# Linear attention of a six-layer decoder: the phi product as two 64-row tiles, in an order one step deeper

## The chip, the cores and the metric

One NeuronCore of one Trainium2 chip runs the whole program. The metric is the device time of one execution in microseconds (us); the time of a kernel is the median of its runs.

## The reference, cut to what matters

A decoder of two blocks works on `x` with 16 sequences of 128 tokens and 128 features. Six layers follow each other, each with a layer norm before it and a residual after it: softmax self-attention, softmax cross-attention, a butterfly feed-forward, linear attention (`_L1_attn_ref`, the layer of this case), autocorrelation cross-attention, and a mixture of experts.

The linear attention has 8 heads of 64 features. It is a recurrence with a decay `g` per head:

```python
q = _phi(x @ W_Q.T); k = _phi(x @ W_K.T)      # _phi(u) = elu(u) + 1
v = x @ W_V.T                                 # all reshaped to (b, t, H=8, DK=64)
S = g4 * S + einsum('bhi,bhj->bhij', kt, vt)  # one step per token
z = g3 * z + kt
out = einsum('bhij,bhi->bhj', S, qt) / (sum(z * qt) + EPS)
...
gate = sigmoid(x @ W_g_w.T + W_g_b)
return (outputs * gate).reshape(b, t, H * DK) @ W_O.T
```

## The kernel before

The kernel computes the recurrence in closed form. For each sequence and head, `A[s, t] = phi_k[s] . phi_q[t]`, multiplied by a mask that holds `g^(t-s)` where t is at least s and zero elsewhere; the numerator is then a matmul of the masked `A` with `v`, to which a column of ones is added so that the denominator comes out as the 65th column.

The stage (`linear_attention`) walks over the 16 sequences, one per step. Everything is fp32. TensorE executes each fp32 matmul as two instructions (a transpose through the identity is one), so the counts in the rows are twice the counts in the code.

Features of two heads share the 128 partitions: head 2c is in rows 0 to 63 and head 2c+1 in rows 64 to 127 of chunk c. The phi product uses full 128-row matmuls: `phi_q` has a slot for each of the two heads, `[128, C4, 2, T]`, and the half of the rows that belongs to the other head stays zero from a memset at the start of the stage. So 4 matmuls of 256 moving columns give all 8 heads, and VectorE writes `phi_q` in two pieces of 64 rows.

Each engine has its own order, written out by hand, and semaphores tie them together. In step b TensorE does: `attend(b)` (the phi product), `turn(b+1)` (transpose of the normalised x), `numerator(b)`, `project_kq(b+1)`, `turn_y(b)` (transposes of the divided output), `project_v(b+1)`, `out(b)` (the output projection), `project_g(b+1)`. VectorE does: `decay(b)` (masking of A, two pieces), `divide(b)`, `gate(b)`, `phi(b+1)`, `prepare(b+2)` (layer norm), `finish(b)` (residual and statistics). ScalarE does the copies and activations of one step after the other: copy of nT, clip and exp for k, the same for q, copy of v, and four tanh for the gate.

The two PSUM banks 4 and 5 hold A, and after it the transposed y and the output projection (`bank_y, bank_z = core.bank[4:6]`); `attend(b)` therefore waits in its second half for `x_done` of step b-1. Banks 6 and 7 hold the numerators.

The mask is built in the first stage (`attention`), in the order of the heads, and multiplied by the triangle there. That stage is the source of some rows below too: in `shifted_scores` (L588) it multiplies operands of 32 rows each, four row groups in turn, each into a bank of its own.

Of the kernel before, what the change touches and what calls it, by code (L numbers as in the profile page):

```python
# [21 lines left out]
B = 16  # L22
T = 128
# [125 lines left out]
def attention(core, m, f, lin, a):  # L149
# [63 lines left out]
    with nc.Block() as block:  # L213
# [164 lines left out]
        def _(act):  # L378
# [458 lines left out]

class LinMem:
# [12 lines left out]
def linear_attention(core, m, au, a):  # L851
# [15 lines left out]
    bank_y, bank_z = core.bank[4:6]  # L867
# [6 lines left out]
    with ExitStack() as ctx:  # L874
# [8 lines left out]
        phi_q = sb("li_phi_q", [128, C4, 2, T])  # L883
# [7 lines left out]
        with nc.Block() as block:  # L891
# [5 lines left out]
            def _(dve):  # L897
                def prepare(b):
# [59 lines left out]
                prepare(0)  # L958
                dve.memset(phi_q[:, :, :, :], 0.0).then_inc(zeroed, 1)
# [3 lines left out]
                dve.wait_ge(zeroed, 2)  # L963
                phi(0)
                prepare(1)
                with dve.Fori(0, B // 2 - 1) as i:
                    step(2 * i)
                    step(2 * i + 1)
                step(B - 2, left=1)
                variance(core, dve, EARLY, next_var)  # L970
                step(B - 1, left=0)
                dve.wait_ge(stat, B)
# [8 lines left out]
            @block.scalar  # L981
            def _(act):
                def prepare(b, first=False):
                    act.wait_ge(turned, b + 1)
                    act.activation(nT[:, :], bank_v[:, 0:T], ACT.Copy).then_inc(n_copied, 1)
                    for i, (proj, bank, clip, ex) in enumerate(((k_proj, bank_k, clip_k, exp_k),
                                                                (q_proj, bank_q, clip_q, exp_q))):
# [4 lines left out]
                        act.activation(ex[:, :, :], clip[:, :, :], ACT.Exp, scale=-1.0).then_inc(raised, 1)  # L992
                    act.wait_ge(v_proj, b + 1)
                    if first:
                        act.wait_ge(zeroed, 2)
                    act.activation(v[:, :, 0:K4], bank_v[:, :].rearrange("p (h w) -> p h w", h=H4), ACT.Copy)\
                        .then_inc(v_copied, 1)
                    act.wait_ge(gate_proj, b + 1)
# [7 lines left out]
                prepare(0, first=True)  # L1006
                with act.Fori(1, B) as b:
                    prepare(b)

            @block.tensor  # L1010
            def _(pe):
                def turn(b):
                    pe.wait_ge(normed, b + 1)
# [21 lines left out]
                def attend(b, first=False):  # L1035
                    pe.wait_ge(phi_done, 3 * (b + 1))
                    for c in range(C4):
                        if c == C4 // 2 and not first:
                            pe.wait_ge(x_done, b)
                        mm = pe.matmul(bank_a[c // 2][:, 256 * (c % 2):256 * (c % 2) + 256], phi_k[:, c, :],  # L1040
                                       phi_q[:, c, :, :].rearrange("p r t -> p (r t)"), start=True, stop=True)
                        if c % 2:
                            mm.then_inc(a_done, 1)

                def numerator(b):
                    pe.wait_ge(v_copied, b + 1)
                    for h in range(H4):
                        if h % half == 0:
                            pe.wait_ge(decayed, 2 * b + h // half + 1)
                        i = h % half  # L1050
                        mm = pe.matmul(bank_num[h // half][:, i * V1:(i + 1) * V1], am[:, h, :], v[:, h, :],  # L1051
                                       start=True, stop=True)
# [16 lines left out]
                def step(b, first=False, last=False):  # L1069
                    attend(b, first)  # L1070
                    if not last:
                        pe.wait_ge(v_copied, b + 1)
                        turn(b + 1)
                    numerator(b)
                    if not last:
                        project_kq(b + 1)
                    turn_y(b)
                    if not last:
                        project_v(b + 1)
                    out(b)  # L1080
                    if not last:
                        project_g(b + 1)

                pe.wait_ge(m.loaded, 80)
                turn(0)
                project_kq(0)
                project_v(0)
                project_g(0, first=True)
                step(0, first=True)
                with pe.Fori(1, B - 1) as b:  # L1090
                    step(b)
                step(B - 1, last=True)
# [1010 lines left out]
```

## Time and profile before

| what | value |
|---|---|
| median of 3 runs | 612.64 us (612.61, 612.64, 618.45) |
| the profiled execution's own time | 617.73 us |
| its span, first to last instruction | 615.6 us |
| busy TensorE, VectorE, ScalarE, GpSimd, of the span | 79%, 56%, 39%, 34% |
| mean granted TensorE clock | 0.875 |

The span is 2.1 us shorter than the profiled execution's own time; the rest lies around the first and last instruction. The profiled execution is 5.1 us above the median, and near to the third run. In the rows, "PE" is TensorE's matmuls, "PEld" its weight loads, "DVE" VectorE, "ACT" ScalarE. A granted clock of 1.00 is 2.4 GHz and 0.50 is 1.2 GHz.

### The profile page before, as it was taken

To read this page: it belongs to the slowest core of one execution; us is meant where nothing else is said; L and a number is where in the kernel's file an instruction comes from. 1 tells how busy PE (TensorE), PEld (TensorE's weight loads), DVE (VectorE), ACT (ScalarE), POOL (GpSimd) and SP (SyncE) were. 2 spreads that over 40 slices of the span, in tenths; PEclk is the share of its full clock that TensorE was granted. 3 is DMA by queue.
4 is the path that set the end of the run, shared out by engine and by line. 5 is a ranking of instruction groups with operands and counts; after the bars stand their busy time and mean duration, and the time that the engine had idled before them with its cause. 6 is when DMAs were issued, how large, how long until landed. Compare 5 with 4: busy or idle time off the path is not lost. (4 is left out here: it accounts for less than half of the span.)

```text
span 615.6 us, 13186 instructions
## 1 busy us (share of the span) xinstructions
PE 485.4 (79%) x4975; PEld 383.4 (62%) x4975; DVE 345.1 (56%) x934; ACT 239.0 (39%) x514; POOL 209.2 (34%) x234
## 2 busy tenths in 40 slices
PE   3879999999977979999999997996275232399960
PEld 1567777777754767888888886875155221266640
DVE  6546777777653446667766764344783767211114
ACT  3756666666542325444543541221121000132313
POOL 3546777799132233000000002123621000447750
PEclk9799999999996989999999997997585555599995
DMA  8960312200000011000000001200006000324417
GB/s 234 394 260 4 113 64 73 68 4 2 4 1 1 0 36 44 1 0 0 0 0 0 0 0 25 63 17 0 1 7 199 1 0 0 94 63 126 121 33 205
DMA packets 31460, 34.71 MB, mean 56 GB/s; under 512 B 5561, under 2 KB 25078, under 8 KB 31288
## 3 DMA queue, kind: packets, MB, share of 16 engines
q1 hardware_dynamic: 29208, 29.50, 15.3%
q0 software_dynamic: 2064, 4.60, 2.3%
q8 instruction: 31, 0.51, 0.4%
q14 instruction: 13, 0.11, 0.1%
q10 hardware_dynamic: 144, 0.00, 0.0%
HBM read 28.65 MB, written 5.46 MB: 55 GB/s over the span
## 5 line engine op out<-in xcount | busy, mean ns | idle before, releaser
L473 DVE TENSOR_REDUCE at_nmax<-bank 128x4 bf16<-128x512 f32 x128 | 82.5, 686 | 48.1 <-PE bank L569 48.1
L413 ACT ACTIVATE at_p<-bank 128x512 f32<-128x512 f32 x128 | 69.3, 597 | 38.2 <-PE bank L588 38.2
L95 POOL TENSOR_TENSOR var<-var,eps 128x12 f32<-128x12 f32 (+1 forms) x8 | 1.7, 206 | 191.1 <-DVE var L88 191.1
L1869 POOL DMA_INDIRECT mo_rows<-mo_n_rows,mo_src_row x24 | 23.0, 959 | 71.2 <-POOLq L1577 64.2
L582 PE MATMUL bank<-ident_b,at_nmax 128*128 128x128 bf16 x512 | 42.9, 222 | 3.9 <-DVE at_nmax L473 3.4
L582 PEld LDWEIGHTS bank<-ident_b,at_nmax 128*128 128x128 bf16 x512 | 31.0, 98 | 18.8 <-issue 9.5
L608 PE MATMUL bank<-at_p,at_v 128*32 128x128 f32 x1024 | 35.0, 276 | 3.9 <-issue 3.0
L1942 ACT ACTIVATE mo_h<-bank,mo_b 128x308 f32<-128x308 f32 x32 | 16.5, 517 | 47.1 <-PE bank L1905 47.1
L1913 PE MATMUL bank<-mo_w,mo_h 128*128 128x128 f32 (+1 forms) x192 | 32.9, 294 | 1.3 <-ACT mo_h L1942 1.3
L1040 PE MATMUL bank<-li_phi_q,li_phi_k 128*128 128x256 f32 x128 | 31.9, 393 | 0.9 <-DVE li_phi_q L908 0.9
L1051 PEld LDWEIGHTS bank<-li_v,li_am 128*128 128x128 f32 x256 | 29.8, 192 | 3.7 <-DVE li_am L915 3.1
L1051 PE MATMUL bank<-li_v,li_am 128*128 128x65 f32 x256 | 31.7, 277 | 0.1
L1913 PEld LDWEIGHTS bank<-mo_w,mo_h 128*128 128x128 f32 (+1 forms) x192 | 24.0, 172 | 11.9 <-ACT mo_h L1942 5.3
L608 PEld LDWEIGHTS bank<-at_p,at_v 128*32 128x32 f32 x1024 | 26.2, 110 | 8.1 <-issue 3.3
L1961 DVE COPY mo_xT<-bank 128x308 f32<-128x308 f32 x8 | 3.8, 478 | 48.2 <-PE bank L1896 48.2
L1637 PE MATMUL bank<-ro_reached,ro_ones_b 128*128 128x56 bf16 x160 | 10.9, 228 | 24.0 <-DVE ro_reached L1733 24.0
L1877 POOL DMA_INDIRECT mo_planes<-mo_y,mo_dst_row x24 | 23.7, 986 | 16.9 <-DVE mo_y L1968 10.5
L282 POOL TENSOR_TENSOR at_k_j<-at_kT,at_mask 128x512 f32<-128x512 f32 x16 | 16.6, 1039 | 30.7 <-PE bank L588 27.5
L1040 PEld LDWEIGHTS bank<-li_phi_q,li_phi_k 128*128 128x128 f32 x128 | 23.0, 190 | 4.3 <-DVE li_phi_q L908 1.1
L1002 ACT ACTIVATE li_tanh<-bank,li_gate_bias 128x128 f32<-128x128 f32 x64 | 18.2, 367 | 19.2 <-PE bank L1018 19.1
L989 ACT ACTIVATE li_clip_k<-bank 128x512 f32<-128x512 f32 x16 | 9.6, 597 | 40.3 <-PE bank L1018 40.3
L1637 PEld LDWEIGHTS bank<-ro_reached,ro_ones_b 128*128 128x128 bf16 x160 | 8.2, 121 | 26.7 <-DVE ro_reached L1733 25.4
(279 smaller groups left out, 1214.5 us busy)
## 6 DMA issues: line engine op xcount, KB each, us to landing
fo_w<-in_up_stages SPq DMA_DIRECT2D x9, 512.0 KB, 9.3
fo_w<-in_down_stages SPq DMA_DIRECT2D x9, 512.0 KB, 4.7
at_k_ctx<-in_ctx_heads SPq DMA_DIRECT2D x1, 4096.0 KB, 21.5
mo_w<-in_L_ffn_W SPq DMA_DIRECT2D x16, 256.0 KB, 3.1
mo_planes<-ro_zeros POOLq DMA_DIRECT2D x1, 2048.0 KB, 9.1
mo_got<-mo_planes SPq DMA_DIRECT2D x8, 256.0 KB, 4.8
x<-in_x SPq DMA_DIRECT2D x4, 256.0 KB, 3.5
au_ctx<-in_ctx SPq DMA_DIRECT2D x4, 256.0 KB, 4.0
```

The source lines that it names most:

```text
L282: pool.tensor_tensor(m.k_j[:, s % K_SLOTS, :, :], over(m.kT[:, g % 2, s % Q, :], J), m.mask[:, :].unsqueeze(2).to_broadcast([D, J, T]), AL ...
L413: act.activation(m.p[:, s % 2, J * g:J * g + J, :], bank_t[g][:, :].rearrange("p (j t) -> p j t", j=J), ACT.Exp, scale=scale).then_inc(exp ...
L473: dve.tensor_reduce(m.nmax[:, J * g:J * g + J], bank_s[g % 2][:, :].rearrange("p (j t) -> p j t", j=J), AX.X, ALU.max, negate=True).then_i ...
L582: pe.matmul(bank_t[g][:, j * T:(j + 1) * T], m.nmax[:, h:h + 1].to_broadcast([T, T]), core.ident_b[:, :], start=(j == 0), stop=False, skip ...
L608: mm = pe.matmul(bank_o[32 * c:32 * c + 32, half * T:half * T + T], m.v[:, g % 2, s % Q, h, :], m.p[:, s % 2, h, :], start=(odd == 0), sto ...
L1002: ins = act.activation(tanh[:, c, :], bank_g[:, c * T:(c + 1) * T], ACT.Tanh, bias=m.gate_bias[:, c:c + 1], scale=0.5)
L1040: mm = pe.matmul(bank_a[c // 2][:, 256 * (c % 2):256 * (c % 2) + 256], phi_k[:, c, :], phi_q[:, c, :, :].rearrange("p r t -> p (r t)"), st ...
L1051: mm = pe.matmul(bank_num[h // half][:, i * V1:(i + 1) * V1], am[:, h, :], v[:, h, :], start=True, stop=True)
L1637: mm = pe.matmul(bank_c[:, 0:TRIALS * E6], ones_b[:, :], reached[:, b, :, :].rearrange("t j e -> t (j e)"), start=(b == 0), stop=(b == B - 1))
L1869: pool.indirect_dma_start(out=rows[0:m, e % 2, r, :], out_offset=None, in_=n_rows, in_offset=bass.IndirectOffsetOnAxis(ap=src_row[0:m, til ...
L1877: pool.indirect_dma_start(out=planes, out_offset=bass.IndirectOffsetOnAxis(ap=dst_row[0:m, tile:tile + 1], axis=0), in_=y[0:m, e % 2, r, : ...
L1913: mm = pe.matmul(bank_y[r][0:m, 0:D], h[:, c, at[r]:at[r] + m], w2[:, par, c, :], start=(c == 0), stop=(c == CH6 - 1))
```

## The change

`phi_q` loses its zero half. Each head has a matmul of its own whose two operands lie in 64 of the 128 rows, 8 matmuls of 128 moving columns in place of 4 of 256; the even heads (rows 0 to 63) go to bank 4 and the odd ones to bank 5, in turn. VectorE writes `phi_q` in one piece of 128 rows, and the memset of it is gone. The masked A, the mask (also where the first stage makes it) and the numerator's order follow the new slots: even heads first, then odd ones. A signals once instead of twice.

The order is one step deeper: the gating, the output projection and the residual of step b-1 are done in step b. TensorE: `attend(b)`, `out(b-1)`, `project_kq(b+1)`, `numerator(b)`, `project_v(b+1)`, `project_g(b+1)`, `turn_y(b)`, `turn(b+2)`. VectorE: `gate(b-1)`, `decay(b)`, `finish(b-1)`, `prepare(b+2)`, `phi_k_of(b+1)`, `divide(b)`, `phi_q_of(b+1)`. ScalarE copies nT of the next step ahead of the gate's tanh. y's transposes and the output projection move to banks 6 and 7, so the numerator now waits for `x_done`. VectorE's loop has one step per turn where it had two.

```diff
@@ attention, scalar
-                act.activation(lin.mask[:, h, :], lin.gap[:, :], ACT.Exp, scale=lin.decay[:, h:h + 1])\
+                act.activation(lin.mask[:, slot(h), :], lin.gap[:, :], ACT.Exp, scale=lin.decay[:, h:h + 1])\
@@
+def slot(h):
+    return (h % 2) * C4 + h // 2
@@ linear_attention
-    bank_y, bank_z = core.bank[4:6]
+    bank_y, bank_z = core.bank[6:8]
-        phi_q = sb("li_phi_q", [128, C4, 2, T])
+        phi_q = sb("li_phi_q", [128, C4, T])
@@ vector
-                def phi(b):
+                def phi_k_of(b):
                     dve.wait_ge(raised, 2 * b + 1)
                     dve.scalar_tensor_tensor(out=phi_k[:, :, :], in0=by_chunk(bank_k[:, :]), scalar=0.0,
                                              in1=exp_k[:, :, :], op0=ALU.max, op1=ALU.add).then_inc(phi_done, 1)
+                def phi_q_of(b):
                     dve.wait_ge(raised, 2 * b + 2)
-                    for r in range(2):
-                        rows = slice(64 * r, 64 * r + 64)
-                        dve.scalar_tensor_tensor(out=phi_q[rows, :, r, :], in0=by_chunk(bank_q[rows, :]), scalar=0.0,
-                                                 in1=exp_q[rows, :, :], op0=ALU.max, op1=ALU.add)\
-                            .then_inc(phi_done, 1)
+                    dve.scalar_tensor_tensor(out=phi_q[:, :, :], in0=by_chunk(bank_q[:, :]), scalar=0.0,
+                                             in1=exp_q[:, :, :], op0=ALU.max, op1=ALU.add).then_inc(phi_done, 1)
                 def decay(b):
+                    dve.wait_ge(a_done, b + 1)
                     for i in range(2):
-                        dve.wait_ge(a_done, 2 * b + i + 1)
...
-                def step(b, left=2):
+                def step(b, first=False, left=2):
+                    if not first:
+                        gate(b - 1)
                     decay(b)
-                    divide(b)
-                    gate(b)
-                    if left >= 1:
-                        phi(b + 1)
+                    if not first:
+                        finish(b - 1)
                     if left >= 2:
                         prepare(b + 2)
-                    finish(b)
-                dve.memset(phi_q[:, :, :, :], 0.0).then_inc(zeroed, 1)
+                    if left >= 1:
+                        phi_k_of(b + 1)
+                    divide(b)
+                    if left >= 1:
+                        phi_q_of(b + 1)
...
@@ tensor
-                def attend(b, first=False):
-                    pe.wait_ge(phi_done, 3 * (b + 1))
+                def attend(b):
+                    pe.wait_ge(phi_done, 2 * (b + 1))
                     for c in range(C4):
-                        if c == C4 // 2 and not first:
-                            pe.wait_ge(x_done, b)
-                        mm = pe.matmul(bank_a[c // 2][:, 256 * (c % 2):256 * (c % 2) + 256], phi_k[:, c, :],
-                                       phi_q[:, c, :, :].rearrange("p r t -> p (r t)"), start=True, stop=True)
-                        if c % 2:
-                            mm.then_inc(a_done, 1)
+                        for r in range(2):
+                            rows = slice(64 * r, 64 * r + 64)
+                            mm = pe.matmul(bank_a[r][:, c * T:(c + 1) * T], phi_k[rows, c, :], phi_q[rows, c, :],
+                                           start=True, stop=True)
+                    mm.then_inc(a_done, 1)
-                def numerator(b):
+                def numerator(b, first=False):
                     pe.wait_ge(v_copied, b + 1)
-                    for h in range(H4):
-                        if h % half == 0:
-                            pe.wait_ge(decayed, 2 * b + h // half + 1)
+                    if not first:
+                        pe.wait_ge(x_done, b)
+                    for r in range(2):
+                        pe.wait_ge(decayed, 2 * b + r + 1)
+                        for h in range(r, H4, 2):
...
+                def step(b, first=False, left=2):
+                    attend(b)
+                    if not first:
+                        out(b - 1)
+                    if left >= 1:
                         project_kq(b + 1)
+                    numerator(b, first)
+                    if left >= 1:
+                        project_v(b + 1)
+                        project_g(b + 1)
                     turn_y(b)
+                    if left >= 2:
+                        turn(b + 2)
```

## Rows read from the trace of the kernel before

**Rows 1.** The page: granted TensorE clock in 40 slices, in tenths of full speed.
```profile
PEclk9799999999996989999999997997585555599995
```

**Rows 2.** Busy time by window: linear attention, routing, experts; then clock, DMA share, GB/s.
```profile
226.00:379.00 153.00, 147.42 (x1008) 126.80 (x1008) 99.50 (x238) 69.19 (x161) 10.05 (x11) 0.97 0.03 8
...
470.00:530.00 60.00, 19.10 (x219) 15.01 (x217) 39.41 (x117) 2.39 (x4) 1.05 (x1) 0.50 0.07 22
530.00:616.00 86.00, 57.15 (x280) 37.61 (x280) 16.39 (x52) 21.66 (x48) 45.63 (x47) 0.84 0.39 111
```

**Rows 3.** Timeline of TensorE's matmuls, one step: start, length, engine, line, operation.
```profile
297.77 2.00 PE L1040 MATMUL bank<-li_phi_q,li_phi_k 128*128 128x256 f32 x8
299.60 0.27 PE L1014 MATMUL bank<-ident,li_n 128*128 128x128 f32 x1
299.71 1.98 PE L1051 MATMUL bank<-li_v,li_am 128*128 128x65 f32 x16
301.52 1.11 PE L1018 MATMUL bank<-li_nT,li_wk 128*128 128x128 f32 x8
302.46 1.06 PE L1018 MATMUL bank<-li_nT,li_wq 128*128 128x128 f32 x8
303.36 0.60 PE L1058 MATMUL bank<-ident,li_y 128*128 128x128 f32 x4
303.80 1.02 PE L1028 MATMUL bank<-li_wv,li_nT 128*128 128x512 f32 x2
304.74 1.16 PE L1065 MATMUL bank<-li_wo,li_yT 128*128 128x128 f32 x8
305.73 1.06 PE L1018 MATMUL bank<-li_nT,li_wg 128*128 128x128 f32 x8
306.65 0.92 PE L1040 MATMUL bank<-li_phi_q,li_phi_k 128*128 128x256 f32 x3
```

**Rows 4.** Timeline of VectorE in the same step.
```profile
299.80 0.69 DVE L915 TENSOR_TENSOR li_am<-bank,li_mask 128x512 f32<-128x512 f32 x1 [0.17 <-PE bank L1040]
301.72 0.23 DVE L923 TENSOR_SCALAR li_den<-bank 128x4 f32<-128x4 f32 x2 [1.23 <-PE bank L1051]
...
302.22 0.76 DVE L930 TENSOR_TENSOR li_y<-bank,li_inv 128x256 f32<-128x256 f32 x2
304.00 0.69 DVE L937 SCALAR_TENSOR_TENSOR li_yT<-li_tanh,bank 128x512 f32<-128x512 f32 x1 [1.02 <-PE bank L1058]
...
305.20 1.40 DVE L908 SCALAR_TENSOR_TENSOR li_phi_q<-bank,li_exp_q 64x512 f32<-64x512 f32 x2
```

**Rows 5.** Timeline of ScalarE in the same step.
```profile
304.44 0.63 ACT L992 ACTIVATE li_exp_q<-li_clip_q 128x512 f32<-128x512 f32 x1
```

**Rows 6.** Timeline of TensorE in the step that holds VectorE's loop boundary.
```profile
272.66 0.27 PE L1014 MATMUL bank<-ident,li_n 128*128 128x128 f32 x1
272.90 2.00 PE L1051 MATMUL bank<-li_v,li_am 128*128 128x65 f32 x16
```

**Rows 7.** Timeline of TensorE in the cross-attention, where row and column tiles are used.
```profile
152.03 1.27 PE L588 MATMUL bank<-at_q,at_k_ctx 32*128 32x128 f32 x32
153.23 1.08 PE L608 MATMUL bank<-at_p,at_v 128*32 128x128 f32 x32
154.24 0.33 PE L612 MATMUL bank<-ident,at_o 128*128 128x128 f32 x1
154.50 0.40 PE L569 MATMUL bank<-at_k_ctx,at_q 32*128 32x512 bf16 x2
```

**Rows 8.** Timeline at the start of the linear attention: the memset and the first phi product.
```profile
226.93 0.91 DVE L959 MEMSET li_phi_q<- 128x1024 f32 x1 [0.16 <-issue]
...
235.02 1.99 PE L1040 MATMUL bank<-li_phi_q,li_phi_k 128*128 128x256 f32 x8 [0.91 <-DVE li_phi_q L908]
```

**Rows 9.** Timeline at its end: the sixteenth phi product (its first instruction) and the last residual.
```profile
369.24 0.48 PE L1040 MATMUL bank<-li_phi_q,li_phi_k 128*128 128x256 f32 x1
...
377.89 0.29 DVE L943 TENSOR_TENSOR x<-bank,x 128x128 f32<-128x128 f32 x1 [1.86 <-PE bank L1065]
```

More of the change, by code:

```diff
@@ L897, in _, with prepare @@
             def _(dve):
-                def prepare(b):
+                def prepare(b, first=False):
+                    if not first:
+                        dve.wait_ge(turned, b)
                     normalise(core, dve, n[:, :], b).then_inc(normed, 1)
-                def phi(b):
+                def phi_k_of(b):
                     dve.wait_ge(raised, 2 * b + 1)
@@ L962, in _ @@
                 dve.wait_ge(s_rstd, 2)
-                dve.wait_ge(zeroed, 2)
-                phi(0)
+                dve.wait_ge(zeroed, 1)
+                phi_k_of(0)
                 prepare(1)
-                with dve.Fori(0, B // 2 - 1) as i:
-                    step(2 * i)
-                    step(2 * i + 1)
+                phi_q_of(0)
+                step(0, first=True)
+                with dve.Fori(1, B - 2) as b:
+                    step(b)
                 step(B - 2, left=1)
@@ L971, in _ @@
                 step(B - 1, left=0)
+                gate(B - 1)
+                finish(B - 1)
                 dve.wait_ge(stat, B)
@@ L982, in _, with turn, features @@
             def _(act):
-                def prepare(b, first=False):
+                def turn(b):
                     act.wait_ge(turned, b + 1)
                     act.activation(nT[:, :], bank_v[:, 0:T], ACT.Copy).then_inc(n_copied, 1)
+                def features(b):
                     for i, (proj, bank, clip, ex) in enumerate(((k_proj, bank_k, clip_k, exp_k),
@@ L992, in prepare, with values, gates @@
                         act.activation(ex[:, :, :], clip[:, :, :], ACT.Exp, scale=-1.0).then_inc(raised, 1)
+                def values(b, first=False):
                     act.wait_ge(v_proj, b + 1)
                     if first:
-                        act.wait_ge(zeroed, 2)
+                        act.wait_ge(zeroed, 1)
                     act.activation(v[:, :, 0:K4], bank_v[:, :].rearrange("p (h w) -> p h w", h=H4), ACT.Copy)\
                         .then_inc(v_copied, 1)
+                def gates(b, first=False):
                     act.wait_ge(gate_proj, b + 1)
@@ L1004, in prepare @@
                     ins.then_inc(tanhed, 1)
-                prepare(0, first=True)
-                with act.Fori(1, B) as b:
-                    prepare(b)
+                turn(0)
+                features(0)
+                values(0, first=True)
+                turn(1)
+                gates(0, first=True)
+                with act.Fori(1, B - 1) as b:
+                    features(b)
+                    values(b)
+                    turn(b + 1)
+                    gates(b)
+                features(B - 1)
+                values(B - 1)
+                gates(B - 1)
             @block.tensor
@@ L1012, in turn @@
                 def turn(b):
+                    pe.wait_ge(v_copied, b)
                     pe.wait_ge(normed, b + 1)
@@ L1033, in project_g @@
                     project(b, m.wg, bank_g, gate_proj)
-                def attend(b, first=False):
-                    pe.wait_ge(phi_done, 3 * (b + 1))
+                def attend(b):
+                    pe.wait_ge(phi_done, 2 * (b + 1))
                     for c in range(C4):
-                        if c == C4 // 2 and not first:
-                            pe.wait_ge(x_done, b)
-                        mm = pe.matmul(bank_a[c // 2][:, 256 * (c % 2):256 * (c % 2) + 256], phi_k[:, c, :],
-                                       phi_q[:, c, :, :].rearrange("p r t -> p (r t)"), start=True, stop=True)
-                        if c % 2:
-                            mm.then_inc(a_done, 1)
-                def numerator(b):
-                    pe.wait_ge(v_copied, b + 1)
-                    for h in range(H4):
-                        if h % half == 0:
-                            pe.wait_ge(decayed, 2 * b + h // half + 1)
-                        i = h % half
-                        mm = pe.matmul(bank_num[h // half][:, i * V1:(i + 1) * V1], am[:, h, :], v[:, h, :],
-                                       start=True, stop=True)
+                        for r in range(2):
[4 more added lines that the diff above has]
+                def numerator(b, first=False):
+                    pe.wait_ge(v_copied, b + 1)
+                    if not first:
[3 more added lines that the diff above has]
+                        for h in range(r, H4, 2):
+                            i = h % half
+                            mm = pe.matmul(bank_num[h // half][:, i * V1:(i + 1) * V1], am[:, slot(h), :], v[:, h, :],
+                                           start=True, stop=True)
                     mm.then_inc(num_done, 1)
@@ L1067, in out @@
                     mm.then_inc(out_done, 1)
[L1069 to L1075, printed above, removed]
+                def step(b, first=False, left=2):
+                    attend(b)
+                    if not first:
+                        out(b - 1)
+                    if left >= 1:
                         project_kq(b + 1)
+                    numerator(b, first)
+                    if left >= 1:
+                        project_v(b + 1)
+                        project_g(b + 1)
                     turn_y(b)
[L1078 to L1082, printed above, removed]
+                    if left >= 2:
+                        turn(b + 2)
                 pe.wait_ge(m.loaded, 80)
-                turn(0)
+                pe.wait_ge(normed, 1)
+                pe.transpose(bank_v[:, 0:T], n[:, :], core.ident[:, :]).then_inc(turned, 1)
                 project_kq(0)
@@ L1088, in _ @@
                 project_g(0, first=True)
+                turn(1)
                 step(0, first=True)
-                with pe.Fori(1, B - 1) as b:
+                with pe.Fori(1, B - 2) as b:
                     step(b)
-                step(B - 1, last=True)
+                step(B - 2, left=1)
+                step(B - 1, left=0)
+                out(B - 1)
 NH5 = 16
```

2 lines of the change are left out of this document (1 added, 1 removed).

## The prediction

> **What bounds the kernel now.** I read the windows by stage first. The changed stage lasts 153 us of 615.6, and TensorE is busy for 147.4 of them at a granted clock of 0.97, nearly all of it at the 2.4 GHz level [rows 2]. Then the timeline of TensorE in one steady step. The reader is to look at the starts, not at the lengths: the lengths overlap, and the distance from one start to the next is what TensorE spends. From one phi product to the next it is 306.65 - 297.77 = 8.88 us, made of 1.83 (phi product), 0.11 (turn), 1.81 (numerator), 0.94 + 0.90 (k, q), 0.44 (turn of y), 0.94 (v), 0.99 (out) and 0.92 (gate), with no hole in it [rows 3]. So TensorE's issue is the bound. What a deeper order alone can give back is small: the v projection streams 2 x 512 columns, which by the other rows' rate (0.112 for 128 columns) is 0.85, so 0.09 of its 0.94 is TensorE waiting for the gating (304.00 to 304.69, and the output projection starts at 304.74 [rows 3, 4]); out takes 0.99 where the equal q projection takes 0.90. Together 0.18 per step. In every second step the numerator starts 0.24 instead of 0.11 after the turn [rows 6]; that is the step with VectorE's loop boundary, where masking comes late. Over the stage, 15 steps from 235.02 to 369.24 [rows 8, 9] are 8.95 each, so this costs 0.07 in the mean.
>
> **The phi product.** Before: 8 instructions of 256 columns, 1.83, or 0.229 each. After: 16 instructions of 128 columns in 64 rows. No row of before shows a 64-row tile. Nearest is the 32-row tile of the cross-attention: 32 instructions, 128 fp32 columns each, and 1.20 us from their first to the next group, 0.0375 each [rows 7]; a full-height instruction of the same columns takes 0.112 [rows 3]. Four row groups in turn therefore do run beside each other. In that group each row tile has 32 / 4 = 8 instructions behind each other, as each of the two 64-row tiles will have (16 / 2). Free overlap would make it 8 x 0.112 = 0.90, the lower bound; the 32-row group takes 1.20, or 1.05 without the one change of tile shape in it (0.15, below). Upper bound, no overlap at all: 16 x 0.112 = 1.79. I take 1.00, nearest to the row, since two tiles have half as many instructions to issue as four.
>
> **The change of tile shape.** The new phi product stands between full-height matmuls, so each step has two changes of shape. The transpose L612 takes 0.26 to its successor, a 32-row tile [rows 7], while the transpose in the linear stage takes 0.11 [rows 3]: 0.15 for a change. I take 0.13 each, 0.26 per step; bounds 0 and 0.35. The Trainium skill, "TensorEngine Tiling (Array Packing)", Key Properties, says that changing the tiling mode, not just the tile, drains TensorE; this is the rule that speaks against the change, and the trace agrees, with the 0.15 above. The same skill, "TensorE: Matmul & The Clock Gate", Packing small matmuls, puts the further tiles of a packed group at about 4 ns each; by that the phi product would be near the floor of 0.90 and the total 1.5 us lower. The trace is above it: 1.05 for the 32-row group without its change, where 0.90 would be free.
>
> **TensorE's step after.** 8.88 - 1.83 - 0.18 + 1.00 + 0.26 = 8.13, against 8.95 in the mean. 0.82 saved, 15 steps: **12.3 us**.
>
> **Does anything else take its place?** I follow the new order with the rows' distances, counting from TensorE's end of the numerator. VectorE's divide starts 0.20 later and its y is done at 302.98, 1.46 after [rows 3, 4]. TensorE has v and gate to issue in that time, 0.85 + 0.92 = 1.77, so turn of y finds y ready with 0.3 to spare. Then phi_q, now one piece of 0.70 instead of two (1.40 [rows 4]), is done at about 2.15 plus some 0.05 of signalling; TensorE wants it after turn of y and turn, at 1.77 + 0.44 + 0.11 = 2.32. Slack 0.1: the tightest place. The output projection needs the gating: turn of y ends its issue at 2.21, its result reaches VectorE some 0.2 later, gating takes 0.69, so 3.15 against 2.32 + 1.26 = 3.58 for TensorE. Masking: a_done at about 3.8, two pieces of 0.69, 5.2; the numerator is reached at 3.58 + 0.90 + 1.84 = 6.3. The residual behind it is ready at 5.5 to 5.8. The exps for q end 3.6 after the k projection's start (305.07 - 301.52) [rows 3, 5], and VectorE takes them 3.65 + 1.46 = 5.1 after it. VectorE's loop boundary, now in each step, lies between phi_q and the gating, where 0.4 is free. v's copy is awaited by turn(b+2), with 0.5 free. The waits that change add none; behind a late phi_q would be the whole TensorE queue. The mask's new slots in the first stage, the other numbering of A and the two banks cost nothing: same instructions, same sizes. ScalarE's copy of nT is done 0.5 after turn; TensorE has phi product and out (2.2) in between.
>
> **The ends.** The first phi product waited for two pieces of phi_q and now for one: 0.7 earlier. The memset of 0.91 is gone, but the first phi_k waits for ScalarE long after it [rows 8], so nothing for that. Step 0 has no output projection: 0.9 less. The last step pays: before, from the sixteenth phi product to the last residual, 8.65 [rows 9]. Now out(14) lies in it, and the numerator waits for its residual, which stands behind two maskings on VectorE with nothing on TensorE to cover it: +1.0. Sum -0.6. **Total -12.9 us.** For the profiled execution that is a span of 602.7 and an own time of 604.8. The median is 5.1 below the profiled execution's time, and the rows don't say where that lies; I take the same 12.9 off the median: 612.64 - 12.9 = 599.7, say 600.
>
> **Rivals.**
> *A, the forecast:* tiles overlap, TensorE's issue stays the bound: 597 to 603.5. Lower end: phi product 0.90, changes 0.2: step 7.97, 2.4 below. Upper: 1.10 and 0.35, step 8.32, 2.9 above.
> *A', phi_q becomes the last to come.* If divide or phi_q is 0.3 later than counted (for instance two signals more), the loop of numerator, divide, phi_q, phi product, out, k and q is 8.4: 604. For it: slack is only 0.1. Against: each part is taken from a row.
> *B, the tiles don't overlap.* The phi product is 1.79 + 0.26, the step 8.92, the stage the same as before within 0.5 and the ends 0.6: 612. The change then doesn't do what it says, and the deeper order only pays for the shape changes. Against it: the 32-row rate; for it: weights of 64 rows and 128 columns are a form that no row shows.
> *C, slower.* Every change from one 64-row tile to the other costs what a change of shape costs. There are 7 inside the phi product: 7 x 0.15 = 1.05 on top of B gives a step of 9.97 and +15 us, 628. The point from which it decides: above 8.95 - 7.05 + 0.18 = 2.08 for the whole phi product with its changes, 0.13 per instruction, the change loses. Against it: L588 changes its row group every second instruction and takes 0.0375 each [rows 7].
> *D, the late stages take another clock.* Routing ran at 0.50 and the experts at 0.84 in the profile [rows 1, 2]; runs of one kernel differ by 5.8 us (612.61 to 618.45), which may be such a change. If most runs of the new kernel fall to that side, 600 + 5.8 = 606.
>
> **How the numbers follow.** A 0.65, A' 0.08, D (with A) 0.09, B 0.12, C 0.06. A measurement here tells about 1% (6.1 us) from no change. Faster by over 1% (below 606.5): A, A' and most of D, 0.80. Within 1%: B and the rest of D, 0.13. Slower: C and a little more, 0.07. The range reaches from A's lower end to D: 596.5 to 607; B and C are left out.
>
> **What would show it.** Right: starts of the phi product 8.0 to 8.3 apart with no wait in TensorE above 0.1; from the phi product's start to out's start 1.1 to 1.4; its matmuls in the form 64*128; VectorE waiting before the gating and before the divide, not TensorE. No alternation from step to step. Wrong: a TensorE wait on phi_q (A'); 1.9 or more from phi product to out (B), over 2.1 (C); a difference that lies behind the end of the stage (D).

## The result and the profile after

| | before | after |
|---|---|---|
| median of the runs beside each other | 613.15 us (612.61 to 618.45) | 599.51 us (598.51 to 600.22) |
| ratio | | 0.974, 95% interval 0.968 to 0.980 |
| profiled execution: own time, span | 617.73, 615.6 us | 599.32, 597.2 us |

The medians are 13.6 us apart, 2.2%; the ratio, which is not formed from the medians, gives 2.6%. The forecast was 600 us. The changed kernel was run again beside the later experiments: 599.98 us against 613.65, ratio 0.980 (0.975 to 0.984).

The windows of the changed kernel, from the profile of that second run (same columns as [rows 2]; linear attention, then routing and experts). The borders are those of [rows 2], 17.5 us earlier from the end of the changed stage on:

```profile
222.50:361.50 139.00, 134.25 (x1136) 120.12 (x1136) 86.06 (x222) 70.78 (x161) 10.13 (x11) 0.95 0.03 9
...
452.50:512.50 60.00, 19.19 (x220) 15.13 (x218) 39.42 (x117) 2.39 (x4) 1.04 (x1) 0.50 0.07 21
512.50:598.00 85.50, 57.24 (x280) 37.66 (x280) 16.41 (x52) 21.66 (x48) 45.62 (x48) 0.84 0.39 113
```

TensorE is still busy for nearly all of the changed stage. The late stages have the clocks that they had before (0.50 and 0.84).

One steady step of TensorE in the changed kernel's first profile; it answers to [rows 3]:

```profile
300.80 1.16 PE L1069 MATMUL bank<-li_phi_q,li_phi_k 64*128 64x128 f32 x16
301.89 1.16 PE L1095 MATMUL bank<-li_wo,li_yT 128*128 128x128 f32 x8
302.89 1.06 PE L1047 MATMUL bank<-li_nT,li_wk 128*128 128x128 f32 x8
303.78 1.06 PE L1047 MATMUL bank<-li_nT,li_wq 128*128 128x128 f32 x8
304.68 1.90 PE L1081 MATMUL bank<-li_v,li_am 128*128 128x65 f32 x16
306.41 1.08 PE L1057 MATMUL bank<-li_wv,li_nT 128*128 128x512 f32 x2
307.32 1.05 PE L1047 MATMUL bank<-li_nT,li_wg 128*128 128x128 f32 x8
308.21 0.60 PE L1088 MATMUL bank<-ident,li_y 128*128 128x128 f32 x4
308.65 0.27 PE L1043 MATMUL bank<-ident,li_n 128*128 128x128 f32 x1
308.85 0.49 PE L1069 MATMUL bank<-li_phi_q,li_phi_k 64*128 64x128 f32 x4
```

The step is 308.85 - 300.80 = 8.05 us, and so in 13 of the 15 steps (the first, without an output projection, is 7.16, and the last, without a turn, 7.94), where before it was 8.95 in the mean [rows 8, 9]. The phi product holds TensorE for 1.09 instead of 1.83. Look at the small differences as well. The numerator takes 1.73 and not 1.81, v 0.91 and not 0.94, gate 0.89 and not 0.92; there TensorE had waited a little in before. k takes 0.89 and not 0.94, but that was no wait. Taken singly, the first instruction of the group behind the numerator has 0.05 more to its successor than it has elsewhere: in before that group is k (0.16 where the others have 0.11), here it is v (0.48 where v's first had 0.43 in before). The 0.05 has only moved to another group.

On the other side, out takes 1.00 where q, the same amount of work, takes 0.90, and turn takes 0.20 where it took 0.11. Those two stand on either side of the 64-row tiles. Out took 0.99 in before too, behind a wait for the gating [rows 3, 4]; here it waits for nothing, and experiment 1 has it at 0.89 with full-height tiles and no wait.

VectorE around the same place; it answers to [rows 4]:

```profile
298.56 0.23 DVE L929 TENSOR_SCALAR li_den<-bank 128x4 f32<-128x4 f32 x2 [0.64 <-PE bank L1081]
...
299.06 0.76 DVE L936 TENSOR_TENSOR li_y<-bank,li_inv 128x256 f32<-128x256 f32 x2
299.74 0.68 DVE L915 SCALAR_TENSOR_TENSOR li_phi_q<-bank,li_exp_q 128x512 f32<-128x512 f32 x1
300.80 0.69 DVE L943 SCALAR_TENSOR_TENSOR li_yT<-li_tanh,bank 128x512 f32<-128x512 f32 x1 [0.39 <-PE bank L1088]
302.01 1.29 DVE L921 TENSOR_TENSOR li_am<-bank,li_mask 128x512 f32<-128x512 f32 x2 [0.52 <-PE bank L1069]
```

phi_q ends at 300.42 (299.74 + 0.68) and the phi product that needs it starts at 300.80. VectorE now waits for TensorE before the divide, the gating and the masking (the brackets), and TensorE waits for no one.

**Where the time went, by stretch.** From the first layer norm of the stage to that of the next stage, the first profile of before has 152.6 us (226.4 to 379.0), the changed kernel 137.9 (222.4 to 360.3) in its first profile and 139.0 in its second. Of that, the 15 steps between the sixteen phi products are 134.22 before and 119.76 after in both: -14.46. The stretch ahead of the first phi product is 8.6 before, 6.8 and 7.95 after; the first of these two ran its first projections at a granted clock of 1.00 and the second at 0.66 at the start, like before. The stretch behind the sixteenth is 9.8 before and 11.3 after. With the second profile, whose start has the clock of before, that is -14.46 - 0.67 + 1.5 = -13.6, the difference of the medians.

The spans of the two first profiles differ by 18.4, not by 13.6: 4.0 of it lie ahead of the changed stage, which begins at 226.4 and at 222.4. The change touches only the order of the mask's slots there, and two of the experiments, which do nothing else to that part, have the 4 us as well (last section).

### The profile page after: what moved, and what is told of

Same layout as the page of the kernel before. It is cut to its first block and busy times, and to the rows that moved or that the text cites. A ratio compares the mean times of both kernels' runs of the same rounds, so it can differ in the third digit from the quotient of the medians.

```text
span 597.2 us, 13480 instructions
## 1 busy us (share of the span) xinstructions
PE 469.0 (79%) x5103; PEld 374.5 (63%) x5103; DVE 332.1 (56%) x917; ACT 240.4 (40%) x514; POOL 209.2 (35%) x234
## 5 line engine op out<-in xcount | busy, mean ns | idle before, releaser
L1081 PE MATMUL bank<-li_v,li_am 128*128 128x65 f32 x256 | 30.4, 272 | 0.5 <-issue 0.5
L921 DVE TENSOR_TENSOR li_am<-bank,li_mask 128x512 f32<-128x512 f32 x32 | 20.6, 686 | 8.7 <-PE bank L1069 8.6
L1938 PE MATMUL bank<-mo_xT,mo_w 128*128 128x308 f32 x64 | 24.7, 492 | 0.6 <-DVE mo_xT L1994 0.6
L588 PE MATMUL bank<-at_q,at_k_j 32*128 32x128 f32 x512 | 21.6, 286 | 0.1
```

What stands on the lines that cost most here:

```text
L588: mm = pe.matmul(bank_t[g][:, j * T:(j + 1) * T], keys(s, g)[:, j, :], queries(s, g), start=False, stop=(j == J - 1), skip_group_check=True)
L921: dve.tensor_tensor(am[:, half * i:half * i + half, :], bank_a[i][:, :].rearrange("p (h t) -> p h t", h=half), m.mask[:, half * i:half * i ...
L1938: pe.matmul(bank_up[c % 2][:, 0:CAP], w1[:, par, c * 128:(c + 1) * 128], xT[:, :], start=True, stop=True).then_inc(up_done, 1)
```

## The experiments

Steps are distances between phi products, as above, from each kernel's profile.

**1. The order alone.** The old full-height product, with the zeros in phi_q and its two pieces, in the new order:

```diff
-                    dve.scalar_tensor_tensor(out=phi_q[:, :, :], in0=by_chunk(bank_q[:, :]), scalar=0.0, ...
+                    for r in range(2):
+                        rows = slice(64 * r, 64 * r + 64)
+                        dve.scalar_tensor_tensor(out=phi_q[rows, :, r, :], in0=by_chunk(bank_q[rows, :]), ...
...
+                        mm = pe.matmul(bank_a[c // 2][:, 256 * (c % 2):256 * (c % 2) + 256], phi_k[:, c, :],
+                                       phi_q[:, c, :, :].rearrange("p r t -> p (r t)"), start=True, stop=True)
```

> The deeper order with the old full-height phi product (phi_q with its zero half, written in two pieces). Theory 1 (each part needs the other): phi_q now stands behind the divide, and in two pieces it comes 0.7 us later than in the changed kernel, where it has 0.33 to spare; TensorE waits about 0.4 per step for it. Step 6.87 + 1.83 + 0.45 = 9.15 us against 8.95 before, time 615 to 617 us. Theory 2 (the parts add up, TensorE's issue bounds): the order alone gives back its 0.18 + 0.07 per step, step 8.70, time 609 to 610 us, no wait on phi_q.

Measured: 616.66 us against 613.9, ratio 1.006 (1.002 to 1.009). Step 9.07. The timeline of TensorE:

```profile
283.88 0.27 PE L1047 MATMUL bank<-ident,li_n 128*128 128x128 f32 x1
284.47 1.99 PE L1071 MATMUL bank<-li_phi_q,li_phi_k 128*128 128x256 f32 x8 [0.32 <-DVE li_phi_q L917]
286.30 1.05 PE L1098 MATMUL bank<-li_wo,li_yT 128*128 128x128 f32 x8
287.19 1.06 PE L1051 MATMUL bank<-li_nT,li_wk 128*128 128x128 f32 x8
```

Theory 1 holds: the deeper order without the one-piece phi_q makes the kernel slightly slower, since VectorE's second piece comes late in every step. This profile also gives the clean price of all the other work, with full-height tiles around it and no wait in it. From turn to the phi product it is 0.59, of which 0.11 are turn itself and 0.48 are lost; 9.07 - 1.83 - 0.48 = 6.76.

One thing stays open here. In every kernel with the full-height product, phi_q comes late or only just in time, and the product's first instruction has 0.32 to its successor where the others have 0.216. So up to 0.10 of the 1.83 may be lateness too; no kernel shows the full-height product with phi_q well ahead of it.

**2. The tiles alone.** The 64-row product and the one-piece phi_q in the old order:

```diff
+                    if not first:
+                        pe.wait_ge(x_done, b)
+                    for c in range(C4):
+                        for r in range(2):
+                            rows = slice(64 * r, 64 * r + 64)
+                            mm = pe.matmul(bank_a[r][:, c * T:(c + 1) * T], phi_k[rows, c, :], phi_q[rows, c, :],
+                                           start=True, stop=True)
+                    mm.then_inc(a_done, 1)
```

> The two 64-row tiles and the one-piece phi_q in the old order. Theory 1: the phi product is done 0.7 us sooner, but the numerator behind it has only one transpose as cover and waits for the masking: from the start of the phi product 1.21 to the mask, 0.69 for its first piece, so the numerator starts 1.94 after, as before. Step 8.88, time 610 to 613 us; the timeline shows TensorE waiting some 0.7 per step before the numerator. Theory 2 (parts add up): 1.83 becomes about 1.2, step 8.30, time 603 to 604 us, no such wait.

Measured: 614.54 us against 613.9, ratio 1.003 (0.999 to 1.006). Step 8.99.

```profile
284.88 1.16 PE L1043 MATMUL bank<-li_phi_q,li_phi_k 64*128 64x128 f32 x16
285.97 0.33 PE L1015 MATMUL bank<-ident,li_n 128*128 128x128 f32 x1
286.83 2.00 PE L1053 MATMUL bank<-li_v,li_am 128*128 128x65 f32 x16 [0.53 <-DVE li_am L917]
```

The phi product is as short as in the changed kernel (1.09), and all of it is given back at once: the numerator starts 1.95 after it, as it did in before (1.94 [rows 3]), because it waits for the masking. That is theory 1 in its mechanism; the step came out 0.11 longer than it said and the time above its 610 to 613, and 0.07 of that is the change of shape in front of the product (gate takes 0.99 here, 0.92 in before). So neither half of the change gains anything; both together gain 13.6 us. The order hides the masking, and phi_q in one piece comes early enough for the order to run without a wait.

**3. Where does 1.09 come from: two tiles beside each other, or cheaper matmuls?**

```diff
-                    for c in range(C4):
-                        for r in range(2):
+                    for r in range(2):
+                        for c in range(C4):
```

> The changed kernel with the phi product's matmuls in another order: the four of rows 0 to 63 first, then the four of rows 64 to 127. Theory 1 (the gain is two row tiles running beside each other, and TensorE issues in order): no overlap, 16 x 0.112 + 0.2 = 2.0 us per phi product in place of 1.09, step 8.95, time 612 to 614 us. Theory 2 (a 64-row matmul is simply cheaper): 1.09 stays, 599 to 600 us.

Measured: 608.5 us against 613.9, ratio 0.991 (0.988 to 0.994). Step 8.60.

```profile
297.75 1.71 PE L1069 MATMUL bank<-li_phi_q,li_phi_k 64*128 64x128 f32 x16
299.38 1.16 PE L1095 MATMUL bank<-li_wo,li_yT 128*128 128x128 f32 x8
```

1.63: neither theory. The same 16 instructions cost 0.54 more when the row group changes once instead of each time, so the gain is overlap and theory 2 falls. But it is 0.35 less than no overlap at all (16 x 0.112 + 0.19 = 1.98), so part of the second group ran beside the first.

The single records show which part. In the changed kernel the starts come in pairs, 0.006 apart, and the pairs follow each other by 0.112 (the first pair by 0.213). Here they begin 0, 0.214, 0.325, 0.437, 0.549 and then 0.555, 0.660, 0.768, 0.772: the fifth instruction of the first row group starts at 298.294, and one that is as long (0.37) as only the first of a row group is starts at 298.300. So the second row group began with three instructions of the first still to start, and 3 x 0.112 = 0.34 fits the 0.35. A record doesn't name its row group; I read it from the lengths and distances.

**4. The row group changes after every second matmul.**

```diff
-                    for c in range(C4):
-                        for r in range(2):
+                    for r, c in ((0, 0), (0, 1), (1, 0), (1, 1), (0, 2), (0, 3), (1, 2), (1, 3)):
```

> The changed kernel with the row group changing after every second matmul (two of rows 0 to 63, two of rows 64 to 127, and again), where the changed kernel alternates each time and the grouped variant changed once. The grouped product took 1.63 us, between 1.09 with full overlap and 2.0 with none. Theory 1 (TensorE starts matmuls of the other row group some instructions ahead of its turn, three in the grouped variant): three boundaries give enough overlap, the product stays at 1.1 to 1.2, step 8.05 to 8.15, time 599.5 to 601 us. Theory 2 (only the neighbouring matmul at a boundary overlaps, two instructions each): 10 instructions behind each other, 1.3, step 8.27, time 603 us.

Measured: 602.06 us against 613.65, ratio 0.983 (0.980 to 0.986). Step 8.15, product 295.10 - 293.91 = 1.19:

```profile
293.91 1.26 PE L1069 MATMUL bank<-li_phi_q,li_phi_k 64*128 64x128 f32 x16
295.10 1.16 PE L1095 MATMUL bank<-li_wo,li_yT 128*128 128x128 f32 x8
```

Theory 1, at the upper end of its step and 1 us above its time: matmuls of the other row group start some instructions ahead of their turn, but only so far. Alternating by one is best, by two costs 0.10, by four 0.54. In the single records the first instruction of the second row group starts here 0.013 behind the first of all; a pair of matmuls has four instructions, so again three of the first row group were still to start. Three instructions is the reach in both variants; whether other sizes or types of matmul have the same is not known.

**5. The product without its changes of tile shape.** Twice the product in a row:

```diff
-                    for c in range(C4):
+                    for c in [*range(C4), *range(C4)]:
```

> The changed kernel with the phi product issued twice in a row (the second writes the same values again). It measures the product without its two changes of tile shape. Theory 1 (8 instructions behind each other per tile at 0.112, and about 0.13 for each change of shape): one more product costs 0.90 to 1.00, step 8.95 to 9.05, time 613.5 to 615.5 us. Theory 2 (changes of shape are free, the product itself takes 1.09 or more): step 9.14 or more, 616.5 us or more.

Measured: 615.25 us against 613.9, ratio 1.002 (0.999 to 1.006). Step 8.95.

```profile
296.16 0.27 PE L1043 MATMUL bank<-ident,li_n 128*128 128x128 f32 x1
296.36 2.06 PE L1069 MATMUL bank<-li_phi_q,li_phi_k 64*128 64x128 f32 x32
298.35 1.16 PE L1095 MATMUL bank<-li_wo,li_yT 128*128 128x128 f32 x8
299.34 1.06 PE L1047 MATMUL bank<-li_nT,li_wk 128*128 128x128 f32 x8
```

1.99 - 1.09 = 0.90, and 8.95 - 8.05 = 0.90: one more product costs exactly 8 x 0.112. That is theory 1, but for its 0.13 per change of shape: two row tiles run wholly free of each other. The rest of the 1.09, and the 0.09 of turn and 0.10 of out, are the two changes of shape: 0.38 per step. By the single records each change costs 0.09 ahead of it (the last instruction of the old shape has 0.20 to its successor) and 0.10 behind it (the first of the new shape has 0.21 to the next).

**6. Two more changes of shape.** The transpose moves from ahead of the phi product into its middle:

```diff
                     for c in range(C4):
+                        if c == C4 // 2 and inside:
+                            turn(b + 1)
...
                     turn_y(b)
-                    if left >= 2:
-                        turn(b + 2)
```

> The changed kernel with the full-height transpose turn(b+1) moved from the end of the step before into the middle of the phi product: two more changes of tile shape per step, nothing else added. Theory 1 (a change of shape costs 0.1 to 0.15): step 8.05 + 0.2 to 0.3, time 603 to 604.5 us. Theory 2 (changes of shape are free, the 1.09 is all product): 599 to 600 us.

Measured: 607.17 us against 613.51, ratio 0.990 (0.985 to 0.994). Step 8.40.

```profile
300.20 0.72 PE L1071 MATMUL bank<-li_phi_q,li_phi_k 64*128 64x128 f32 x8
300.84 0.33 PE L1043 MATMUL bank<-ident,li_n 128*128 128x128 f32 x1
301.10 0.72 PE L1071 MATMUL bank<-li_phi_q,li_phi_k 64*128 64x128 f32 x8
301.75 1.16 PE L1097 MATMUL bank<-li_wo,li_yT 128*128 128x128 f32 x8
```

Two more changes, the same work: 0.35 per step, 0.17 each. The trace shows no wait at either of them, so the price is that of the change itself. Theory 2 falls, and theory 1 had the price too small: it said 0.2 to 0.3 per step and 603 to 604.5 us. 15 x 0.35 = 5.3 would give some 605 us; the lowest of the four runs was 605.39 and the median is 2 above. The profiled execution (610.3) is 11.0 above that of the changed kernel: 3.6 ahead of the stage (last section), 5.9 in it and 1.5 behind it. Whether the other three runs have the same additions is not known.

**7. How close is phi_q?** One VectorE operation more ahead of it, then two; each takes 0.33 us to the next and writes a tile that nothing reads:

```diff
                 def phi_q_of(b):
                     dve.wait_ge(raised, 2 * b + 2)
+                    dve.tensor_scalar(spare[:, :], exp_q[:, :, :].rearrange("p c t -> p (c t)"), 0.0, None, ALU.max)
```

> The changed kernel with one more VectorE operation per step between divide and phi_q (it writes exp_q's 128 x 512 elements into a spare tile that nothing reads). In the changed kernel's timeline phi_q has 0.33 us to spare. Theory 1 (TensorE's issue bounds, with phi_q 0.33 behind it): the step grows by the operation's length less 0.33, for 0.6 us by about 0.27, time 603 to 604 us, and TensorE waits for phi_q by that. Theory 2 (my slack of 0.1 in the prediction was right): it grows by the length less 0.1, 606 to 607 us. Theory 3 (phi_q is not close to the bound): 599 to 600 us.

> The changed kernel with two more VectorE operations per step (each writes 128 x 512 elements into a spare tile that nothing reads) between divide and phi_q, where the variant with one (0.33 us) cost nothing. Theory 1 (phi_q has 0.33 us to spare, and behind that TensorE waits for it one for one): 0.66 - 0.33, the step grows by 0.33 to 0.36 to 8.4, time 604 to 605.5 us, TensorE waits for phi_q in each step. Theory 2 (phi_q has a larger cover): 599 to 600 us.

Measured: with one 599.66 us against 613.51, ratio 0.979 (0.974 to 0.983), step 8.05; with two 607.2 us against 613.65, ratio 0.992 (0.988 to 0.996), step 8.39, and TensorE waits in each step:

```profile
296.71 0.27 PE L1046 MATMUL bank<-ident,li_n 128*128 128x128 f32 x1
297.25 1.16 PE L1072 MATMUL bank<-li_phi_q,li_phi_k 64*128 64x128 f32 x16 [0.27 <-DVE li_phi_q L918]
```

The cover of phi_q is one such operation, 0.33 us, and behind it TensorE pays one for one: +0.34 for the second. With one operation theories 1 and 3 foresee the same, and only the second decides for theory 1. Its step came out as forecast, and its median 1.7 above the forecast times; the lowest of its six runs, 605.11, is where 15 x 0.34 would put it.

**8. The order alone, with phi_q brought forward.** Kernel 1 with the first piece of phi_q ahead of the divide:

```diff
                         phi_k_of(b + 1)
+                        phi_q_of(b + 1, (0,))
                     divide(b)
                     if left >= 1:
-                        phi_q_of(b + 1)
+                        phi_q_of(b + 1, (1,))
```

> The deeper order with the old full-height phi product, but the first of phi_q's two pieces written ahead of the divide and the second behind it, so that the last piece comes when the changed kernel's single one does. Theory 1 (the 0.31 that TensorE waits for phi_q in each step is all that kept the order from paying): the wait goes, step 8.76, time 611 to 613 us, some 4.6 us below the variant with the order only. Theory 2 (the divide behind the first piece becomes late instead): step stays at 9.0 or more, 616 us, with TensorE waiting before the transposes of y.

Measured: 613.84 us against 613.65, ratio 0.999 (0.996 to 1.003). Step 8.88, between the theories: 0.19 of the wait went. The rest is at two places:

```profile
299.12 1.05 PE L1052 MATMUL bank<-li_nT,li_wg 128*128 128x128 f32 x8
300.12 0.66 PE L1092 MATMUL bank<-ident,li_y 128*128 128x128 f32 x4
300.61 0.27 PE L1048 MATMUL bank<-ident,li_n 128*128 128x128 f32 x1
300.84 1.99 PE L1072 MATMUL bank<-li_phi_q,li_phi_k 128*128 128x256 f32 x8
```

Here gate to turn of y is 1.00 (0.89 in the changed kernel), turn of y 0.49 (0.44) and turn to phi product 0.23 (0.11 with full-height tiles). The first piece, which waits 0.45 for ScalarE's exps, ends at 298.90 and pushes the divide back by 0.4, and turn of y and phi product are each late by 0.1. The steps can be put into a sum: 9.07 in experiment 1; 6.76 + 1.83 = 8.59 if nothing were late (an estimate from experiment 1, no kernel has it); 8.05 in the changed kernel. So phi_q in time is worth 0.48 per step to the order, of which this variant gets 0.19, and the shorter product with its changes of shape 0.54.

**The changed kernel again.**

> The changed kernel itself, to stand beside the other three on the same chip. Both theories: step 8.05, time 598.5 to 600.5 us; if the wait before the linear attention (4 us longer in some profiles, of either kernel) is a matter of the execution and not of the change, a profile or some runs may be 604 us.

Measured: 599.98 us (597.82 to 602.69), as expected. Step 8.05.

No kernel with both tiles in one PSUM bank was tried, so whether the even-odd numbering of A is needed stays open. None of the experiments beats the changed kernel; what is left in it is the 0.38 per step for the changes of shape, some 6 us in all. With the products of two sequences side by side half of the changes would go, about 3 us by this estimate; that was not tried.

## Why the prediction was right

**The bound.** That TensorE's issue sets the step was right for the changed kernel: no wait stands in its steady step, and lengthening only its work (experiment 5) moves the step by just that. For the kernel before it was half of the truth. There the masking was ready just when TensorE was: the numerator starts 1.94 after the phi product, and with the product 0.74 shorter it starts 1.95 after it (experiment 2). Two paths of the same length bounded that step, and the prediction names one.

**The terms of TensorE's step.** Predicted 7.05 - 0.18 + 1.00 + 0.26 = 8.13, measured 6.76 + 0.90 + 0.38 = 8.04, and 8.05 in the trace. Three sizes were off, by -0.11, -0.10 and +0.12, and two of them cancel; that the sum came within 0.08 is in part luck. The other work is 6.76 and not 6.87: the numerator's 0.08 and gate's 0.02, which I had taken for work, were waits as well. The product is 0.90, the lower bound, and not 1.00: two tiles cost nothing over one, while the cross-attention's group of four row tiles, from which I had taken it, is slower than free. The changes of shape are 0.38 and not 0.26: each costs something ahead of it and something behind it (0.09 and 0.10, experiment 5), and the distance from one transpose to its successor, from which I had taken the price, shows only the part ahead. The range's upper end was 0.35. The Trainium skill's rule ("TensorEngine Tiling (Array Packing)", Key Properties) that a change of mode drains TensorE fits the 0.17 to 0.19 for each. Its rule that a further tile in a packed group costs a few ns ("TensorE: Matmul & The Clock Gate", Packing small matmuls) is borne out by the 0.90 and by the 0.006 between the starts of two tiles, and would have been the better choice there; but the traces have it only where the other tile is at most three instructions away.

**What takes its place.** Nothing did, as predicted. Where I named phi_q as the tightest place with 0.1 to spare, it has 0.33 (experiment 7): phi_q starts 0.68 after y's two pieces begin and not after they end (0.76), v and gate take 1.80 and not 1.77, and turn takes 0.20. So the place was right and its slack was mis-sized. A' fell.

**The rivals.** B fell by experiments 3 and 5, C by 5 (the changes of row group inside the product cost nothing). D did not occur in the profiles: the late stages take 236.9 and 236.3 us behind the changed stage, and 236.6 in before. The profiled execution of before, one of the longer ones that D thought of, has its extra time ahead of the changed stage, where it is 4.0 us behind already (last section). B's sentence that the deeper order "only pays for the shape changes" was wrong in its reason: without the one-piece phi_q it doesn't even do that (experiment 1).

**What I had not seen.** The prediction added the parts up, 0.57 for the tiles (1.83 - 1.00 - 0.26) and 0.25 for the order (0.18 + 0.07). Their sum was right, but experiments 1 and 2 show that neither is there alone. It was right for the sum since the waits were followed through for the two together.

**The ends.** The -14.46 between the phi products holds 0.9 of step 0 and 0.1 of the last step, which lacks a turn; the steps alone gave 15 x (8.95 - 8.05) = 13.5 where 12.3 were forecast. The first phi product comes 0.67 earlier where the clock is the same (predicted 0.7), and step 0 gives its 0.9 (predicted 0.9). The stretch behind the sixteenth is 1.5 longer (predicted 1.0). Half of it is the wait for the residual, there as named: from the phi product to the numerator it is 2.80 (349.00 to 351.80) where it was 2.09 (369.24 to 371.33). The other half was not foreseen: the last transposes and the last projection ran longer, first the changed kernel, then before:

```profile
351.80 1.97 PE L1081 MATMUL bank<-li_v,li_am 128*128 128x65 f32 x16 [0.51 <-issue]
...
355.11 1.12 PE L1088 MATMUL bank<-ident,li_y 128*128 128x128 f32 x4 [1.35 <-DVE li_y L936]
...
357.01 2.07 PE L1095 MATMUL bank<-li_wo,li_yT 128*128 128x128 f32 x8 [0.78 <-DVE li_yT L943]
```

```profile
374.65 0.66 PE L1058 MATMUL bank<-ident,li_y 128*128 128x128 f32 x4 [1.35 <-DVE li_y L930]
376.08 1.76 PE L1065 MATMUL bank<-li_wo,li_yT 128*128 128x128 f32 x8 [0.78 <-DVE li_yT L937]
```

In the changed kernel the granted clock is 1.00 up to 355, 0.53 from 355 to 356 and 0.50 behind that, so both groups run at the lower level; in before it is still 1.00 for the transposes and falls within the projection. The ends together gave about -0.2 (predicted -0.6) and the steps -13.5 (predicted -12.3). Total: predicted -12.9, measured -13.6.

## What to carry to other kernels

Shortening one engine's work and deepening the order can each be worth nothing and together be worth the whole: after each part, ask which result comes last now, and let the next edit remove that wait. In this fp32 stream row tiles paid in full only where the row groups alternate matmul by matmul, and each entry into and exit from a tile shape cost about 0.18 us, half of it on the neighbour; so put work of one shape together. Take the clean price of a piece of work from a step in which nothing is waited for, since waits of up to 0.1 in distances from start to start look like work.

## What the hardware showed that was not expected

**TensorE does not keep row tiles strictly in turn.** With four matmuls of one row group ahead of four of the other, 16 instructions took 1.63 us with their changes of shape, against 1.09 alternating and 1.98 if one followed the other. In both variants that don't alternate by one, the second row group began with three instructions of the first still to start (experiments 3 and 4).

**A wait in the first stage that some profiles have.** Three of the twelve profiles (before, experiments 5 and 6) begin the linear attention at 226.0 to 226.7 us, the other nine at 222.0 to 223.1, whatever the kernel. In those three TensorE stands still once for 2.2 to 3.0 us in the self-attention (and once for 0.4 to 0.9 some 9 us earlier), with nothing that it waits for in the profile; here the waits of its matmuls from 20 to 100 us in before, and the same in the second profile of after:

```profile
PE bank L608 <- issue: 3.0, 1, 3.0
PE bank L582 <- DVE at_nmax L473: 0.4, 2, 0.2
```

```profile
PE bank L582 <- DVE at_nmax L473: 1.1, 5, 0.2
PE bank L582 <- ACT at_p L413: 0.5, 1, 0.5
```

In before it lies from 40.3 to 43.4 us, while the transfers are heavy: the DMA share is 0.62 from 40 to 42 and 0.85 from 42 to 44. But the changed kernel has 0.78 and 0.89 in the same two windows, and TensorE is busy for all of both. What holds TensorE in those three executions was not tested. Two of the three are variants of the changed kernel that leave this stage as it is, so it does not come from the change. For whoever compares two profiled executions it is 4 us that belong to neither kernel. It would explain most of the 5.1 us by which the profiled execution of before lay above its median; the other runs have no profile that could show it.
